# Projections of the local blocks from operands split into a high and a low part, with weights that are parted beside the expert blocks

## What is computed

```
def attn_layer(x, Wqkv, qs, ksc, Wo):
    qkv = x @ Wqkv                        # 128 -> 3 * 1024
    q, k, v = jnp.split(qkv, 3, -1)       # 16 heads of 64
    q = l2norm(q) * qs
    k = l2norm(k) * ksc
    q = q * cos * scale + rotate_half(q) * sin * scale
    k = k * cos / scale + rotate_half(k) * sin / scale
    out = local_attention(q, k, v)        # windows of 32, looks one window back
    return out @ Wo
x = attn_layer(shift_tokens(x), ...) + x ; x = ffn_layer(x, ...) + x     # six times
```

## Time and profile before

| | |
|---|---|
| median of 3 runs | 4556.72 us (4555.56 to 4574.86) |
| the profiled execution | 4564.9 us, its span 4562.7 us |
| PE busy | 4259.3 us, 93% of the span |
| DVE, ACT, POOL busy | 3479.4, 2566.2, 2436.2 us (76%, 56%, 53%) |
| local blocks | about 582 to 2284 us and 2840 to 4555 us of the span |
| PE clock over the span | 0.963 of full speed |

### The profile page before, as it was taken

The page is one execution under the profiler, slowest core; times in us unless marked ns, Lnnn a source line. Parts: engine busy times, 40 slices in busy tenths (PEclk is TensorE's granted clock), DMA queues, the critical chain, the costliest instruction groups (busy, mean ns, idle before and its releaser), DMA issues. The chain is left out here.

```text
span 4562.7 us, 148825 instructions
## 1 busy us (share of the span) xinstructions
PE 4259.3 (93%) x65704; PEld 2746.0 (60%) x65704; DVE 3479.4 (76%) x4359; ACT 2566.2 (56%) x2978; POOL 2436.2 (53%) x3091
## 2 busy tenths in 40 slices
PE   8999979999999999999878887899999999999997
PEld 5655556666666666666533333566666666666664
DVE  4435478888888888888568884888888888888885
ACT  3414345665665656666427774465656666666663
POOL 1001066666766666666324440766667666666673
PEclk8989999999999999999959997999999999999998
DMA  3102032322223222222100000222222222222221
GB/s 102 54 1 82 30 89 56 85 62 77 72 64 80 70 71 74 66 75 70 43 1 1 1 1 30 70 61 79 65 74 75 66 76 70 76 69 74 63 66 51
DMA packets 160209, 272.72 MB, mean 60 GB/s; under 512 B 38280, under 2 KB 42000, under 8 KB 159440
## 3 DMA queue, kind: packets, MB, share of 16 engines
q1 hardware_dynamic: 159568, 263.21, 21.2%
HBM read 66.86 MB, written 1.18 MB: 15 GB/s over the span
## 5 line engine op out<-in xcount | busy, mean ns | idle before, releaser
L651 PE MATMUL psum<-loc_wqkv,loc_zs 128*128 128x512 f32 x2304 | 1122.5, 610 | 21.3 <-DVE loc_zs L1200 15.6
L651 PEld LDWEIGHTS psum<-loc_wqkv,loc_zs 128*128 128x128 f32 x2304 | 404.2, 192 | 374.7 <-issue 331.9
L1006 POOL TENSOR_TENSOR loc_rc_k<-loc_rc_k,loc_rs_k 128x1024 f32<-128x1024 f32 x192 | 454.4, 2367 | 141.9 <-DVE loc_rs_k L1087 141.4
L746 PEld LDWEIGHTS psum<-loc_PT,loc_V 64*64 64x64 f32 x24576 | 394.0, 135 | 197.7 <-issue 196.0
L746 PE MATMUL psum<-loc_PT,loc_V 64*64 64x32 f32 x24576 | 423.9, 220 | 46.9 <-issue 42.3
L884 ACT ACTIVATE loc_sq_k<-psum 128x1024 f32<-128x1024 f32 x192 | 196.6, 1024 | 478.2 <-PE psum L651 478.2
L1006 POOL TENSOR_TENSOR loc_rc_q<-loc_rc_q,loc_rs_q 128x1024 f32<-128x1024 f32 x192 | 453.2, 2360 | 0.0
L765 PEld LDWEIGHTS psum<-loc_outT,loc_wo 128*128 128x128 f32 x3072 | 382.7, 196 | 100.2 <-issue 96.7
L981 POOL TENSOR_TENSOR loc_rt<-loc_rn 128x32 f32<-128x32 f32 x192 | 45.8, 238 | 686.9 <-DVE loc_rn L1083 673.4
L765 PE MATMUL psum<-loc_outT,loc_wo 128*128 128x128 f32 x3072 | 382.9, 279 | 1.9 <-DVE loc_gg L1143 1.9
L1012 POOL TENSOR_TENSOR loc_qk_q<-loc_rc_q,loc_rn 128x1024 f32<-128x1024 f32 x192 | 365.4, 1903 | 27.0 <-issue 0.8
(11 more groups left out here) (181 smaller groups left out, 9057.4 us busy)
## 6 DMA issues: line engine op xcount, KB each, us to landing
loc_V<-loc_V SPq DMA_DIRECT2D x1152, 128.0 KB, 2.3
loc_V<-loc_V SPq DMA_DIRECT2D x672, 64.0 KB, 2.0
loc_wqkv<-in_wqkv SPq DMA_DIRECT2D x42, 512.0 KB, 3.7
moe_spread<-moe_gates SPq DMA_DIRECT2D x64, 256.0 KB, 3.9
moe_w<-in_moe_w SPq DMA_DIRECT2D x32, 256.0 KB, 3.1
loc_wo<-in_wo SPq DMA_DIRECT2D x12, 512.0 KB, 4.3
loc_w<-in_w SPq DMA_DIRECT2D x12, 341.0 KB, 3.3
loc_w<-in_w SPq DMA_DIRECT2D x12, 192.0 KB, 3.4
```

The costliest lines, as they stand in the source:

```text
L651: mm = pe.matmul(M.bank[bank + g], zs[:, s, i * P:(i + 1) * P], wqkv[:, k, g * T:(g + 1) * T], start=True, stop=True)
L746: mm = pe.matmul(M.bank[WB + c][64 * j:64 * j + 64, m * P + q:m * P + q + 32], V2[r:r + 64, i, w, p * 64:(p + 1) * 64], PT[r:r + 64, p, q: ...
L1006: pool.tensor_tensor(rc[:, :], rc[:, :], rs[:, :], ALU.add).then_inc(added, 1)
```

## The change

In the local blocks each projection is made from split operands: `z_hi`, `z_lo` for the tokens, `w_hl` for the weights, three fp32r matmuls where one float32 matmul stood. The tokens of a sequence are split once, in the step where the sequence before is begun or earlier (DVE `cut_tokens`, ACT `round_tokens`, POOL `rest_of_tokens`, one instruction of 512 columns each). The weights of all six layers are split once, 9 chunks of 1024 columns in each expert block (load and subtraction on POOL, cut on DVE), and stored to a DRAM scratch `parted`; the local blocks load them from there, twice the bytes, with transfers that POOL issues and no longer SP. To make room, one buffer `sq` serves both squares, V and V2 keep three tiles in place of four, `xh` is not held during local blocks, and full attention loads its weights at its own start. The layer norm ahead of a local block writes straight into the shifted `zs`, in two instructions of 64 partitions for each sequence; the clearing and the copies are gone.

```diff
@@ layernorm_block
+        if shifted is not None:
+            @block.gpsimd
+            def _(pool):
+                pool.memset(shifted[:, :, 0:1], 0.0).then_inc(opened, 1)
+                pool.memset(shifted[:, :, T:T + 2], 0.0).then_inc(opened, 1)
+                    dve.tensor_tensor(shifted[0:64, s, 0:T], dst[0:64, s * T:(s + 1) * T], RSTD[s % 2][0:64, :], ALU.mult)
+                    dve.tensor_tensor(shifted[64:P, s, 1:T + 1], dst[64:P, s * T:(s + 1) * T], RSTD[s % 2][64:P, :],
+                                      ALU.mult).then_inc(out_ready, 1)
...
@@ expert_block
+    CHUNKS = [(L, k) for L in layers for k in (1, 2, 0)]
+    EVERY = 14
+        def chunk_at(i):
+            c, at = divmod(i, EVERY)
+            return c if at == 10 and c < len(CHUNKS) else None
+            def load_chunk(c):
+                L, k = CHUNKS[c]
+                pool.dma_start(raw[:, c % 2, :], W["wqkv"][L, :, k * INNER:(k + 1) * INNER]).then_inc(raw_loaded[c % 2], 16)
+            def rest_of_chunk(c):
+                pool.wait_ge(chunk_cut, c + 1)
+                pool.tensor_tensor(halves[:, c % 2, 1, :], raw[:, c % 2, :], halves[:, c % 2, 0, :],
+                                   ALU.subtract).then_inc(chunk_split, 1)
+            def store_chunk(c):
+                L, k = CHUNKS[c]
+                pool.wait_ge(chunk_split, c + 1)
+                pool.dma_start(M.parted[L, :, k, :, :], halves[:, c % 2, :, :]).then_inc(chunk_stored[c % 2], 16)
+            for u in range(2):
+                pool.wait_ge(chunk_stored[u], 16 * ((len(CHUNKS) + 1 - u) // 2))
...
@@ local_transformer_block, SP
-                if n == TS - 1 and live(n):
-                    sp.wait_ge(k_full, upto(L, TS - 1))
-                    sp.sem_inc(sp_passed, 1)
-                    load_qkv(L + 1, 1, wk_loaded)
...
@@ local_transformer_block, PE
             def project(bank, t, k, full):
-                s, i = t // TILES % SEQS, t % TILES
+                r, tokens = t // TILES % 2, slice(t % TILES * P, (t % TILES + 1) * P)
                 for g in range(2):
-                    mm = pe.matmul(M.bank[bank + g], zs[:, s, i * P:(i + 1) * P], wqkv[:, k, g * T:(g + 1) * T],
-                                   start=True, stop=True)
+                    cols = slice(g * T, (g + 1) * T)
+                    pe.matmul(M.bank[bank + g], z_lo[:, r, tokens], w_hl[:, k, 0, cols], start=True, stop=False)
+                    pe.matmul(M.bank[bank + g], z_hi[:, r, tokens], w_hl[:, k, 1, cols], start=False, stop=False)
+                    mm = pe.matmul(M.bank[bank + g], z_hi[:, r, tokens], w_hl[:, k, 0, cols], start=False, stop=True)
                 mm.then_inc(full, 1)
...
@@ local_transformer_block, ACT
+            def round_tokens(L, s):
+                act.wait_ge(z_cut, L * SEQS + s + 1)
+                act.activation(z_hi[:, s % 2, :], z_bits[:, :], ACT.Copy).then_inc(z_high, 1)
             def square_q(L, t):
                 act.wait_ge(q_full, upto(L, t))
-                act.wait_ge(q_totalled, upto(L, t - 1))
-                act.activation(sq_q[:, :], W_, ACT.Square).then_inc(q_squared, 1)
+                act.wait_ge(k_totalled, upto(L, t))
+                act.activation(sq[:, :], W_, ACT.Square).then_inc(q_squared, 1)
...
@@ local_transformer_block, POOL
+            def load_parts(L, k, loaded):
+                pool.dma_start(w_hl[:, k, :, :], M.parted[L, :, k, :, :]).then_inc(loaded, 16)
+            def rest_of_tokens(L, s):
+                pool.wait_ge(z_cut, L * SEQS + s + 1)
+                pool.tensor_tensor(z_lo[:, s % 2, :], zs[:, s, 0:T], z_bits[:, :], ALU.subtract).then_inc(z_split, 1)
             def step(L, n, live):
                 if live(n - 5) and lasts(n - 5):
                     deviation(L, n - 5)
+                if n == 0 and 0 < L < DEPTH:
+                    pool.wait_ge(q_full, upto(L, -1))
+                    load_parts(L, 0, wq_loaded)
                 if live(n - 1):
                     root(L, n - 1)
+                if n == TS - 1 and L + 1 < DEPTH:
+                    pool.wait_ge(k_full, upto(L, n))
+                    load_parts(L + 1, 1, wk_loaded)
+                if live(n - 1):
                     scaled(L, n - 1, k_added, tk_full, rc_k, HEADS, qk_k, k_ready)
...
+                if n == TS - 1 and L + 1 < DEPTH:
+                    pool.wait_ge(v_full, upto(L, n))
+                    load_parts(L + 1, 2, wv_loaded)
                 if live(n):
                     total_of(L, n, k_rotated, rc_k, rs_k, k_added)
+                if n % TILES == 2 and L < DEPTH:
...
@@ local_transformer_block, DVE
+            def cut_tokens(L, s):
+                dve.wait_ge(z_ffn, upto_seq(L, s - SEQS))
+                dve.tensor_scalar(z_bits[:, :].bitcast(I32), zs[:, s, 0:T].bitcast(I32), LOW_BITS, None,
+                                  ALU.bitwise_and).then_inc(z_cut, 1)
+                if n % TILES == 0 and L < DEPTH:
+                    after, s = divmod(n // TILES + 1, SEQS)
+                    if L + after < DEPTH:
+                        cut_tokens(L + after, s)
-            dve.memset(zs[:, :, :], 0.0).then_inc(cleared, 1)
-            dve.wait_ge(cleared, 4)
-            x_in = M.xh[:, :].rearrange("p (s n) -> p s n", n=T)
-            dve.tensor_copy(zs[0:64, :, 0:T], x_in[0:64])
-            dve.tensor_copy(zs[64:P, :, 1:T + 1], x_in[64:P]).then_inc(zs_ready, 1)
...
@@ full_attention_block
+            sp.dma_start(wqkk[:, :, :], W["wqkk"].rearrange("p (y n) -> p y n", y=3)).then_inc(qkk_loaded, 16)
+            sp.dma_start(wv_full[:, :], W["wv_full"]).then_inc(v_loaded, 16)
+            sp.dma_start(wo_full[:, :], W["wo_full"]).then_inc(out_loaded, 16)
```

185 lines of the change are left out of this document (117 added, 68 removed).

## The result

The changed kernel takes 4586.38 us (median of 11 runs, 4576.44 to 4608.44), the kernel before 4559.51 us (11 runs beside it). The ratio is 1.006, 95% interval 1.0041 to 1.0078. The forecast was 4446 us, with 0.06 for slower.

A forecast was written before the change was run, and what follows sets the result against it. PE bounds the kernel before; with shorter projections the loop of DVE and POOL would bind. 4564.9 - 142 + 10 + 14 + 4 + 3 = 4454 us, less 8 for the profiled run: 4446 us, range 4395 to 4520.

The forecast's parts named there:

- the loop's length: Local blocks: DVE's guess, POOL's roots and scaled k, DVE's cosine to next guess; 64.64 us for four steps, 16.16 each.
- The term of -142 us: Local blocks: shorter projections bring the step from 17.24 to 16.5 us, 0.74 us gained in each of 192 steps.
- The four-step walk: Four local steps replayed with PE's pieces shortened: the loop of DVE and POOL rules at 16.16 us, PE waiting about 0.25.
- The token split: Local blocks: DVE's cut, ACT's rounding and POOL's subtraction are covered by waits and cost nothing.
- POOL's loads: Layer ends: ten times POOL's issue of a weight load between roots and scaled k costs 1 us; +10 us (3 to 20).
- Block starts: Two local block starts: later first load, +4 us, and longer norm, at most 2.8 us, each; +14 us (4 to 24).
- Full attention: Start of full attention: it waits for its own weight load; +4 us (0 to 8).
- Rival 2: Local blocks: PE's whole saving of 196 us arrives since the loop's legs shrink too; 4392 us, chance 0.08.
- rival 3: Layer starts: weights land late, q by 5 us at ten of them; +50, 4496 us, chance 0.12.
- Rival 4: Boundaries and starts: weight loads take 25 us or more; slower than before, at most 4626 us, chance 0.06.
- Rival 5: Local steps: the wait moves, DVE's legs stretch by 0.7 us a step beside POOL; 4557 us, within 0.5%, chance 0.08.
- my signs for a wrong forecast: Steps above 16.8 us, layer starts above 22 us, or fp32r matmuls spaced wider than 0.25 us with weights as wide operand.

The follow-up runs named there:

- one_pass: Changed kernel with one fp32r matmul (high by high) in each projection where it has three; 4576.32 us, ratio 1.0035 to the kernel before.
- before_small_first: Kernel before with spread, gate, variance and linear half moved ahead of the value matmuls in PE's order; 4542.66 us, ratio 0.9973.
- f32_small_first2: Changed kernel with the small matmuls ahead of the value matmuls and float32 projections from the weights' high part; 4574.03 us, ratio 1.0022 to the kernel before.
- after_small_first: Changed kernel with spread, gate, variance and linear half moved ahead of the value matmuls in PE's order; 4495.02 us, ratio 0.986 to the kernel before.
- split_once: Changed kernel with tokens split only for the first two sequences of each block, later ones reading old parts; 4594.24 us, ratio 1.0067 to the kernel before.
- keep_weights: Changed kernel with layer 0's weights kept for all layers, 30 loads of 1 MB left out; 4583.18 us, ratio 1.004 to the kernel before.
- few_transfers: Changed kernel with one transfer of v a tile in place of eight or ten, V2 cleared whole; 4560.74 us, ratio 1.0014 to the kernel before.

## Why the prediction was wrong

**The step that failed** is the one behind the loop's length: "the four steps took 68.10 us, because in the others DVE waited for PE, 1.91 us for the spread and 2.62 us for a linear half", and from it "the loop rules: 16.16 us", with those waits taken out. I read them as the mark of a full PE that shorter projections would relieve. They end at small matmuls that stand behind the value matmuls in PE's order, and this stretch took back what the projections gave: from the sine's end to the last value matmul it was 3.49 us before, 3.39 after and 3.31 with one pass, by growing pauses and slower matmuls (0.43 us a step in the changed kernel) and, with one pass, by the wait for the sine in 69 steps of 75. DVE's waits stayed at 127.6 us. The term of -142 us came out as (16.97 - 16.98) x 166 = -2 us for the steps inside layers. The two rows of waits stood in the earlier trace rows; what I didn't do was to follow each back over PE to its own releaser. The four-step walk kept two rules (guess plus 5.87 us; turning behind the sine of k), and two were missing: value matmuls no earlier than the sine of q, because both use one bank, and a run of them that gets longer when PE has less wide work.

**"PE is the bound"** was right for the kernel before. PE had 98% of the stretch, in the 1300 us no run of value matmuls was held by the sine, and before_small_first agrees: leg P fell by 0.65 us but leg D grew by 0.54, and the step stayed (16.98 to 16.99). Wrong was what a shorter PE is worth in this order: nothing, while with the small matmuls ahead it is worth a step inside layers of 16.65 us in place of the 17.07 of f32_small_first2.

**Size of the projection's gain.** The spacing of 0.23 us held (1344.09 to 1344.32 in the trace of after). PE lost 1270.93 - 1224.21 = 47 us of busy time in 1300, 0.62 us a step against the 1.02 predicted; the window's clock fell from 0.99 to 0.97, so part of the time came back as slower matmuls. In the new order the gain was 74 us, half of the 142. The loop of DVE and POOL was the limit there, as foreseen, but longer than foreseen: 16.65 us where the prediction had 16.16 without any wait. Its leg D in those 162 steps is 10.71 us against 41.16/4 = 10.29, and the normalisation of the probabilities, one of its instructions, is enough for that: 1.41 us in the four steps that the prediction measured, 1.91 here. By the pages, kernel before and after_small_first, all steps:

```profile
L1115 DVE TENSOR_TENSOR loc_prob<-loc_prob,loc_recip 128x1024 f32<-128x1024 f32 x192 | 304.4, 1586 | 6.6
L1209 DVE TENSOR_TENSOR loc_prob<-loc_prob,loc_recip 128x1024 f32<-128x1024 f32 x192 | 360.6, 1878 | 6.6
```

**The token split** at 0 was right (split_once). **POOL's loads** at +10 us were right in kind and somewhat low: 13 to 16 us against SP's queue, 17 us at the layer ends of keep_weights (its whole time fell by less, within the intervals). They landed in 6.8 us, just below my 7 to 11:

```profile
loc_w_hl<-parted POOLq DMA_DIRECT2D x36, 1024.0 KB, 6.8
```

What I had left out is that a layer's end is itself two long steps (37.85 us before, where two inside take 33.96), so an issue ahead of the scaled k falls where POOL and DVE are late already. **Block starts** at +14 us: POOL issued late and PE waited for the load, as foreseen:

```profile
577.63 1.59 POOL L1032 DMA_DIRECT2D loc_w_hl<-parted  x3 [21.89 <-issue]
...
585.45 0.77 PE L695 MATMUL psum<-loc_w_hl,loc_z_lo 128*128 128x512 f32 x1 [11.81 <-DMA loc_w_hl<-parted]
```

PE began at 585.45 against 581.77, 3.7 us later, and that is all; the first sixteen steps took as long as before. The sum of 14 was too high. **Full attention** at +4 us had the wrong sign: the stretch from the last k square of the first block to the first of the second went from 638.5 to 625.8 us. Near its start the granted clock was higher, 0.74 against 0.54; here are those windows, before and after (the second begins some 12 us later in its work than the first). Why the clock was higher there, no run shows:

```profile
2284.00:2394.00 110.00, 80.66 (x264) 35.85 (x268) 67.90 (x115) 27.16 (x47) 27.81 (x20) 0.54 0.00 1
```

```profile
2310.00:2420.00 110.00, 82.40 (x399) 37.36 (x401) 80.77 (x132) 43.52 (x79) 38.14 (x27) 0.74 0.03 11
```

**The rivals.** Rival 2 (PE's whole saving arrives) and rival 3 (weights late in the layers) did not come true. Rival 4 named the loads, with a price from 11 us a boundary; they cost 1.3 to 1.7. Rival 5 ("moves the wait but not the time") was nearest in time, yet its mechanism, DVE's legs stretching by 0.7 us, is not what happened: leg D grew by 0.11. In the new order it did come in part, by the 0.4 us above. Of my signs for a wrong forecast the first came true, steps above 16.8 us, but none of the rivals held the stretch of value matmuls. That the changed kernel came out behind and not level fits the cost of the surroundings, 22 us in the new order.

## What to carry to other kernels

Where an engine waits for PE, ask which instruction of PE it waits for, what stands ahead of that one in PE's order, and what released it; only work between those two points shortens the wait. A wait for a full engine isn't yet a wait because the engine is full. When a wait stays as long after its engine was relieved, look at the order first: here moving four small matmuls ahead of 64 short ones (no work saved) was worth 91 us, and only then did the cheaper projections count. Test an edit also in the form that takes far too much away (one_pass): if nothing moves, something takes back what the edit gives, and the trace of that extreme form shows it most clearly.

## What the runs showed of the hardware

- PE stops inside runs of short matmuls with no semaphore to wait for, 1 to 3 us at a time: 0.39 us a step before, 0.69 after, 0.91 with one pass, 0.19 with half of the value matmuls, 0.38 with four products. In these kernels it stops the more, the less wide work stands between the short matmuls. Most stops of over 0.3 us began 1 to 2.5 us after the start of a 16 KB transfer of the queue that the page calls "q8 instruction": 64 of 82 before and 74 of 109 after, where such moments make up 22% of the time. That they are waits for instructions is argued from this, not shown; few_transfers, with the share of DMA down from 0.28 to 0.09, still had 0.54 us.
- Where PE was idle more, it had more time at half clock: 0.22 us a step before, 0.92 after, 1.93 with one pass and 0.35 with four products, in the steady parts of the blocks. So PE gave part of what it was spared back in this way.
- A normalisation on DVE (L1115, then L1209), a product of two SBUF operands, went from a mean of 1586 to 1693 ns with more work on POOL beside it, while the cosines, which read PSUM, stayed at 1221 and 1222. The Trainium skill, "SBUF — State Buffer", section "SBUF: two separate sides", has the two engines share a port; these numbers agree. In the old order, at 0.1 us a step, it decided nothing; in the new one, with a mean of 1878 ns, it lengthens the loop that rules.
